# Attention scores: VectorE subtracts for all eight heads, ScalarE takes one exponential per graph

## The chip, the cores and the metric

One Trainium2 chip, one core. The metric is the device time of one launch in microseconds (us). The kernel before was timed three times; the profile is of a fourth execution.

## What is computed

There are 128 graphs of 128 nodes with 128 channels each. A graph layer with attention comes first, then a mixture of experts; the change lies in the attention alone.

```python
q, k, v = (split_heads(layernorm(x) @ W + b) for W, b in ((Wq, bq), (Wk, bk), (Wv, bv)))   # 8 heads of 16
scores = einsum('bhqd,bhkd->bhqk', q, k) / 4
scores = where(adj[:, None] > 0, scores, -9e15)
attn = softmax(scores, axis=-1)
x = x + (attn @ v, heads joined) @ Wo + bo
x = x + ffn(layernorm(x))        # a shared expert and the best two of eight others
```

## The kernel before

The program has five phases, one behind the other: attention, router, shared expert, routed experts, and a last one that adds the pairs up. The attention phase goes over 128 tiles, one graph each, in 32 rounds of four tiles (`GT = 4`; tile `t = 4g + j`). Every engine has its own list of work, written out by hand in a `step(g, q)` of its own, and the lists meet at semaphores only. Within an engine the order is fixed.

For one tile the work goes like this. TensorE writes the negated scores of eight heads into the four banks of S (L736) and adds the mask with four more matmuls (L739), which raises `s_ps`. VectorE takes the minimum per head (L474, `softmax_shift`, L470) and then subtracts the scores from it for the first `SHIFTED = 6` heads, from PSUM into `probs` in SBUF (L477), which raises `sub_done`. ScalarE computes the other two heads straight from S, one exponential each with the minimum as bias (L621, `direct_done`), and then exponentiates the six shifted heads in place (L626, `exp_done`). TensorE turns the eight blocks in two halves (L750, L766) into the one bank of PT, which ScalarE copies out after each half (L612, L616), and multiplies by V (L778); ScalarE copies the sums (L629), TensorE turns them (L759), and VectorE divides by the denominators (`normalise`, L457).

There is one S. TensorE's step for the next tile begins with the scores into S, and waits for `sub_done` and `direct_done` of the tile before (L732, L733).

Around this each round of four tiles carries other work, at a fixed place behind the subtraction of one of its tiles. On VectorE: at j = 0 `normalise` and the statistics of a later group (`stats1`, `gather1`); at j = 1 `residual` and `choose`; at j = 2 `normalise` and `mask` (L455, the mask of the next group); at j = 3 `place` (L504, whose first product L507 raises `slot_terms`), `stats2` and `gather2`. On TensorE: `aT` at j = 0, `out` at j = 1, Q and K at j = 2, V and the router's logits (`lg`, L705) at j = 3. At j = 3 the product with V waits for `slot_terms`, since the ranks share its bank. On ScalarE: copies of `aT`, Q, K, V and the logits. GpSimd (POOL) normalises rows (L297 and L301 among others) and sends rows to their slots.

Of the kernel before, what the change touches and what calls it, by code (L numbers as in the profile page):

```python
# [20 lines left out]
VW = 2 * HD  # L21
HH = H // 2
NEG = -9000000000000000.0
SHIFTED = 6
EPS = 1e-5
E = 8
EA = E + 1
# [24 lines left out]
def attention_phase(nc, ctx, d, x_res, x_rows, row_words, logits, rt, row_sent, xT_dram, slots_dram):  # L52
# [7 lines left out]
    def sem(name):  # L60
# [69 lines left out]
             "k_ps", "k_sb", "v_ps", "v_sb", "aT_ps", "aT_sb", "out_ps", "x2_done", "bn2_done", "aggr2", "rs1_done", "rs2_done", "ve1_done", "ve2_done", "xc1_done", "xc2_done",  # L130
             "xs2_done", "hi_done", "split_done", "x2T_in", "lg_ps", "lg_sb",
             "top_done", "eq_done", "keyed", "key_done", "pick_done", "rest_done", "rank_ps", "counted", "slot_terms", "slot_ready",
             "s_ps", "min_done", "sub_done", "direct_done", "exp_done", "pt_ps", "pt_sb", "pv_ps", "o_sb", "on_ps", "rec_done", "norm_done"]
    s = {n: sem(n) for n in names}

    def wait(eng, name, count):
# [228 lines left out]
    def _(dve):  # L365
# [104 lines left out]
        def softmax_shift(t, b):  # L470

            wait(dve, "s_ps", t + 1)
            wait(dve, "sub_done", t)
            dve.tensor_reduce(smin[:].rearrange("p (r e) -> p r e", e=2), S_heads, AX_X, ALU.min).then_inc(s["min_done"], 1)  # L474
            wait(dve, "min_done", t + 1)
            wait(dve, "pt_ps", 2 * (t - 1))
            dve.tensor_tensor(probs[:, b, 0:SHIFTED].rearrange("p (r e) k -> p r e k", e=2),  # L477
                              smin[:, 0:SHIFTED].rearrange("p (r e) -> p r e", e=2).unsqueeze(3).to_broadcast([P, SHIFTED // 2, 2, P]),
                              S_heads[:, 0:SHIFTED // 2], ALU.subtract).then_inc(s["sub_done"], 1)

        def choose(g, q):

# [80 lines left out]
    @nc_block.scalar  # L563
    def _(act):
        act.wait_ge(prep, 8)

        def high_half(g):
            wait(act, "xn_ready", g + 1)
            wait(act, "xnT_in", g * GT * 16)
            act.activation(xn16[:, :, 0], xn[:], ACT.Copy).then_inc(s["xhi_done"], 1)  # L570

        def evac(task, g, q):
            if task == "Q":
                wait(act, "q_ps", g + 1)
                act.activation(QT[:, q], M0[:, :], ACT.Identity, bias=qb[:], scale=-0.25 / (XS * WS)).then_inc(s["q_sb"], 1)
            elif task == "K":
                wait(act, "k_ps", g + 1)
                for e in range(2):
                    last = act.activation(KT[:, q, e], M0[:, :], ACT.Identity, bias=kb[:, e:e + 1], scale=parity_s[:, e:e + 1])
                last.then_inc(s["k_sb"], 1)  # L580
            elif task == "V":
                wait(act, "v_ps", g + 1)
                act.activation(V[:, q, :, :, 0:HD].rearrange("p j h c -> p (j h) c"),
                               M0[:, :].rearrange("p (j c) -> p j c", c=HD), ACT.Copy,
                               scale=1.0 / (XS * WS)).then_inc(s["v_sb"], 1)
            elif task == "aT":
                wait(act, "aT_ps", g + 1)
                act.activation(attnT[:], last_bank(g, task)[:, :], ACT.Copy).then_inc(s["aT_sb"], 1)
            elif task == "lg":
                set_up(act, g)  # L590
                wait(act, "lg_ps", g + 1)
                act.activation(logits[:, bass.ds(g * GT, GT), :], M0[:, 0:GT * E].rearrange("p (j e) -> p j e", e=E),
                               ACT.Copy, scale=1.0 / (XS * WS)).then_inc(s["lg_sb"], 1)

        def keep_transposed(t, half):
            wait(act, "pt_ps", 2 * t + half + 1)
            if half == 0:
                wait(act, "pv_ps", t - 1)
            return PT[:, :, :]

        def step(g, q):
            for j in range(GT):
                t = g * GT + j
                b = {0: ("lg", g - 4, q), 1: None, 2: ("Q", g + 1, 1 - q), 3: ("K", g + 1, 1 - q)}[j]
                a = {0: ("aT", g - 2, q), 1: None, 2: None, 3: ("V", g + 1, 1 - q)}[j]
                if isinstance(g, int) and g == -1 and j == 0:
                    high_half(0)
                    high_half(1)
                if b and has(b[1]):
                    evac(*b)  # L610
                if has(t, 1, NT):
                    act.activation(pT[:, (j - 1) % 2, 0:HH], keep_transposed(t - 1, 0), ACT.Copy).then_inc(s["pt_sb"], 1)  # L612
                if a and has(a[1]):
                    evac(*a)
                if has(t, 1, NT):
                    act.activation(pT[:, (j - 1) % 2, HH:H], keep_transposed(t - 1, 1), ACT.Copy).then_inc(s["pt_sb"], 1)  # L616
                if has(t, 0, NT):
                    wait(act, "min_done", t + 1)
                    wait(act, "pt_ps", 2 * (t - 1))
                    for h in range(SHIFTED, H):  # L620
                        last = act.activation(probs[:, j % 2, h], S_heads[:, h // 2, h % 2], ACT.Exp,  # L621
                                              bias=smin[:, h:h + 1], scale=-1.0)
                    last.then_inc(s["direct_done"], 1)
                    wait(act, "sub_done", t + 1)
                    pr = probs[:, j % 2, 0:SHIFTED]
                    act.activation(pr, pr, ACT.Exp).then_inc(s["exp_done"], 1)  # L626
                if has(t, 2, NT):
                    wait(act, "pv_ps", t - 1)
                    act.activation(oT[:], OD[:, 0:2 * P].rearrange("p (a t) -> p a t", a=2), ACT.Copy).then_inc(s["o_sb"], 1)  # L629
                if j == 3 and has(g, -2) and not (isinstance(g, int) and g < 0):  # L630
                    high_half(g + 2)

        def drain():
            evac("lg", NG - 4, 0)
            act.activation(pT[:, 1, 0:HH], keep_transposed(NT - 1, 0), ACT.Copy).then_inc(s["pt_sb"], 1)
            evac("aT", NG - 2, 0)
            act.activation(pT[:, 1, HH:H], keep_transposed(NT - 1, 1), ACT.Copy).then_inc(s["pt_sb"], 1)
            for t in (NT - 2, NT - 1):
                wait(act, "pv_ps", t + 1)
                act.activation(oT[:], OD[:, 0:2 * P].rearrange("p (a t) -> p a t", a=2), ACT.Copy).then_inc(s["o_sb"], 1)  # L640
            evac("aT", NG - 1, 1)
            for g in range(NG - 3, NG):
                evac("lg", g, g % 2)

        pair_blocks(act, step)
        drain()

    @nc_block.tensor
    def _(pe):
# [10 lines left out]
        def m0_task(task, g, q, step_g):  # L660
# [15 lines left out]
            elif task == "aT":  # L676
                wait(pe, "norm_done", (g + 1) * GT // 2)
                bank = last_bank(g, task)
                if bank is not M0:
                    wait(pe, "sub_done", NT)  # L680
                    wait(pe, "direct_done", NT)
                else:
                    m0_free(pe, task, step_g)
                for j in range(GT):
                    mm = pe.transpose(bank[:, j * P:(j + 1) * P], attn[:, q, j].rearrange("p h c -> p (h c)"), ident[:])
                mm.then_inc(s["aT_ps"], 1)
            elif task == "out":
                wait(pe, "aT_sb", g + 1)
                bank = last_bank(g, task)
                if bank is M0:  # L690
                    m0_free(pe, task, step_g)
                pe.matmul(bank[:, :].rearrange("p (j c) -> p j c", j=GT), sel[:],
                          bias3[:].unsqueeze(1).to_broadcast([P, GT, P]), start=True, stop=False)
                for j in range(GT):
                    mm = pe.matmul(bank[:, j * P:(j + 1) * P], attnT[:, j * P:(j + 1) * P], wo[:], start=False, stop=j == GT - 1)
                mm.then_inc(s["out_ps"], 1)
            elif task == "lg":
                rows_turned(pe, g)
                if isinstance(g, int) and g >= NG - 3:
                    wait(pe, "lg_sb", g)  # L700
                else:
                    m0_free(pe, task, step_g)
                for j in range(GT):
                    for n, (a, b) in enumerate(((0, 0), (0, 1), (1, 0))):
                        mm = pe.matmul(M0[:, j * E:(j + 1) * E], xT[:, q, a, j * P:(j + 1) * P],  # L705
                                       wr16[:, b], start=n == 0, stop=n == 2)
                mm.then_inc(s["lg_ps"], 1)
# [13 lines left out]
        def step(g, q):  # L721
            for j in range(GT):
# [4 lines left out]
                if has(t, 0, NT):  # L727
# [2 lines left out]
                        wait(pe, "k_sb", g + 1)  # L730
                        wait(pe, "mask_ready", g + 1)
                    wait(pe, "sub_done", t)  # L732
                    wait(pe, "direct_done", t)  # L733
                    for r in range(4):
                        rows = slice(32 * r, 32 * r + 32)
                        pe.matmul(S_heads[:, r], QT[rows, q, j * P:(j + 1) * P], KT[rows, q, :, j * P:(j + 1) * P],  # L736
# [835 lines left out]
```

## Time and profile before

| what | value |
|---|---|
| median of three runs | 1387.17 us (1382.49 to 1388.42) |
| the profiled execution | 1381.66 us, span 1379.8 us |
| PE, DVE, ACT, POOL busy over the whole span | 79%, 73%, 63%, 62% |
| first and last reduction of scores (L474) | 43.4 us and 657.9 us |

The attention phase is a little under half of the span. Shares over the whole span mix it with four phases that have other limits, so they tell little of it; the round of four tiles is the unit to look at, and the length of a step is the time from one reduction L474 to the next. In the rows, PE is TensorE, PEld its weight loads, DVE VectorE, ACT ScalarE. A bracket at the end of a row of the timeline gives how long the engine was idle before it, and what ended that.

### The profile page before, as it was taken

The page shows a single profiled execution, that of the slowest core. Times are in us where ns is not written, and L with a number is a line of the kernel's source. Part 1 is how long each engine was busy: PE and PEld are TensorE (multiplying, and loading weights), DVE is VectorE, ACT ScalarE, POOL GpSimd, SP SyncE. Part 2 cuts the span into 40 slices and gives each one's busy share as a digit, 9 for nine tenths or more (in the row PEclk, how much of TensorE's full clock was granted, in tenths as well). Part 3 has the DMA queues.
Part 4 walks back from the last instruction along what each step waited for, and adds up shares of the span by engine and source line. Part 5 has one row for each costly group of instructions (what it writes and reads, how often), then busy time and mean ns, then how long its engine had stood idle before and what let it go on. Part 6 is the DMA issues. An engine that isn't in the chain of part 4 may idle for free. (4 is left out here: it accounts for less than half of the span.)

```text
span 1379.8 us, 39795 instructions
## 1 busy us (share of the span) xinstructions
PE 1088.6 (79%) x12580; PEld 791.9 (57%) x12581; DVE 1010.7 (73%) x2407; ACT 866.9 (63%) x1705; POOL 856.1 (62%) x897
## 2 busy tenths in 40 slices
PE   0788888888888888888348999989999999989300
PEld 0456666666666666666226767757777777768200
DVE  3367777777877787777447798767777777757498
ACT  0577777777777777777236878766767676657200
POOL 3125676776667766675666777627777777766400
PEclk9999999999999999999769999999999999989755
DMA  2112333323333223322233545244444444423399
GB/s 74 25 45 65 84 82 84 92 67 82 84 87 81 76 79 86 82 67 49 70 98 102 164 147 156 77 80 103 97 101 97 90 101 96 88 63 77 113 337 307
DMA packets 276549, 136.54 MB, mean 99 GB/s; under 512 B 195142, under 2 KB 254700, under 8 KB 276474
## 3 DMA queue, kind: packets, MB, share of 16 engines
q1 hardware_dynamic: 242938, 93.39, 28.2%
q0 software_dynamic: 16896, 33.86, 7.7%
q10 hardware_dynamic: 16640, 8.39, 2.0%
q8 instruction: 34, 0.56, 0.2%
q14 instruction: 41, 0.34, 0.1%
HBM read 47.95 MB, written 54.04 MB: 74 GB/s over the span
## 5 line engine op out<-in xcount | busy, mean ns | idle before, releaser
L1376 POOL DMA_INDIRECT pairs_dram<-x_rows x272 | 278.9, 1025 | 124.5 <-issue 85.1
L1054 ACT ACTIVATE hid<-Z,biases 128x512 f32<-128x512 f32 (+1 forms) x336 | 208.1, 631 | 138.4 <-PE Z L1022 91.1
L474 DVE TENSOR_REDUCE smin<-S 128x8 f32<-128x1024 f32 x128 | 156.8, 1225 | 136.3 <-PE S L739 135.2
L1069 DVE SCALAR_TENSOR_TENSOR h<-hid,h 128x512 f16<-128x512 f32 (+1 forms) x288 | 183.7, 650 | 53.3 <-ACT h L1045 48.9
L1034 PEld LDWEIGHTS Y<-w,h 128*128 128x128 f16 x3168 | 186.0, 99 | 26.7 <-issue 10.6
L1034 PE MATMUL Y<-w,h 128*128 (+1 forms) x3168 | 193.0, 221 | 10.3 <-DVE h L1069 8.3
L1167 POOL DMA_INDIRECT slots_dram<-x_rows,pair_slot x128 | 132.7, 1036 | 46.0 <-issue 23.9
L1022 PE MATMUL Z<-x_rows,w 128*128 128x512 f16 (+1 forms) x720 | 150.2, 355 | 11.0 <-issue 8.8
L736 PE MATMUL S<-KT,QT 32*128 32x256 f32 x1024 | 93.0, 429 | 75.2 <-ACT probs L621 71.6
L335 POOL DMA_INDIRECT slots_dram<-x_rows,pair_slot x116 | 118.7, 1023 | 28.9 <-issue 23.4
L306 POOL TENSOR_TENSOR xn<-xn 128x512 f16<-128x512 f32 x32 | 37.0, 1156 | 159.9 <-ACT xn L570 159.9
L477 DVE TENSOR_TENSOR probs<-smin,S 128x768 f32<-128x768 f32 x128 | 122.1, 954 | 14.4
L616 ACT ACTIVATE pT<-PT 128x512 f32<-128x512 f32 x127 | 75.7, 596 | 71.1 <-PE PT L766 70.7
L1045 ACT ACTIVATE h<-hid 128x512 f16<-128x512 f32 (+1 forms) x176 | 105.8, 601 | 21.0 <-ACT hid L1054 5.4
L626 ACT ACTIVATE probs<-probs 128x768 f32<-128x768 f32 x128 | 109.3, 854 | 0.4 <-DVE probs L477 0.4
L1034 PE MATMUL Y<-w,x_rows 128*128 x1632 | 101.7, 220 | 6.7 <-DVE x_rows L1429 6.1
L1069 DVE SCALAR_TENSOR_TENSOR x_rows<-hid,x_rows 128x512 f16<-128x512 f32 (+1 forms) x160 | 97.1, 620 | 11.9 <-ACT x_rows L1045 8.9
L1034 PEld LDWEIGHTS Y<-w,x_rows 128*128 128x128 f16 x1632 | 96.6, 98 | 15.9 <-issue 8.6
L1022 PEld LDWEIGHTS Z<-x_rows,w 128*128 x720 | 66.7, 100 | 65.7 <-issue 16.9
L612 ACT ACTIVATE pT<-PT 128x512 f32<-128x512 f32 x127 | 76.5, 603 | 43.7 <-PE PT L750 43.7
L736 PEld LDWEIGHTS S<-KT,QT 32*128 32x128 f32 x1024 | 44.3, 185 | 101.1 <-issue 63.6
L1429 DVE SCALAR_TENSOR_TENSOR x_rows<-Y,logits 128x512 f32<-128x512 f32 (+1 forms) x80 | 48.9, 612 | 66.2 <-DMA pairs_dram<-x_rows 50.3
(212 smaller groups left out, 2244.7 us busy)
## 6 DMA issues: line engine op xcount, KB each, us to landing
y_pairs<-pairs_dram SPq DMA_DIRECT2D x32, 512.0 KB, 6.1
x_res<-in_x_dram SPq DMA_DIRECT2D x32, 256.0 KB, 3.3
adj<-in_adj_dram SPq DMA_DIRECT2D x32, 256.0 KB, 2.9
xT_dram<-xT SPq DMA_DIRECT2D x32, 256.0 KB, 3.3
xTu<-xT_dram SPq DMA_DIRECT2D x32, 256.0 KB
out_dram<-x_res ACTq DMA_DIRECT2D x16, 512.0 KB, 10.8
pairs_dram<-x_rows POOLq DMA_INDIRECT x272
slots_dram<-x_rows,pair_slot POOLq DMA_INDIRECT x256
```

The source lines that it names most:

```text
L335: pool.indirect_dma_start(slots_dram, bass.IndirectOffsetOnAxis(ap=rt.pair_slot[:, g * GT + j, 0:1], axis=0), row_words[:, g * GT + j, :], ...
L474: dve.tensor_reduce(smin[:].rearrange("p (r e) -> p r e", e=2), S_heads, AX_X, ALU.min).then_inc(s["min_done"], 1)
L477: dve.tensor_tensor(probs[:, b, 0:SHIFTED].rearrange("p (r e) k -> p r e k", e=2), smin[:, 0:SHIFTED].rearrange("p (r e) -> p r e", e=2).u ...
L626: act.activation(pr, pr, ACT.Exp).then_inc(s["exp_done"], 1)
L736: pe.matmul(S_heads[:, r], QT[rows, q, j * P:(j + 1) * P], KT[rows, q, :, j * P:(j + 1) * P], start=True, stop=False)
L1022: mm = pe.matmul(self.bank(b, c)[:, 0:w], self.w1[:, k, :, c * P:(c + 1) * P][:, e, :], self.xT[:, b, m, 0:w], start=n == 0, stop=n == 2)
L1034: mm = pe.matmul(self.Y[:, b % 2, j], self.piece(b)[:, k, c, j * P:(j + 1) * P], self.w2[:, m, :, c][:, e, :], start=c == 0 and n == 0, st ...
L1045: act.activation(self.piece(b)[:, 0, c, 0:w], self.hid[:, c, 0:w], ACT.Copy, scale=HS).then_inc(self.hi_done, 1)
L1054: act.activation(self.hid[:, c, 0:w], self.bank(b, c)[:, 0:w], ACT.Gelu, bias=bias[:, c:c + 1], scale=1.0 / (XS * WS)).then_inc(self.gelu_ ...
L1069: dve.scalar_tensor_tensor(out=self.piece(b)[:, 1, c, 0:w], in0=self.hid[:, c, 0:w], scalar=HS, in1=self.piece(b)[:, 0, c, 0:w], op0=ALU.m ...
L1167: pool.indirect_dma_start(slots_dram, bass.IndirectOffsetOnAxis(ap=rt.pair_slot[:, t, k:k + 1], axis=0), row_words[:, t, :], None).then_in ...
L1376: pool.indirect_dma_start(pairs_dram, bass.IndirectOffsetOnAxis(ap=pair_of[n][:, j:j + 1], axis=0), y_sb[n % NY][:, j], None, bounds_check ...
```

## The change

The two direct exponentials go. VectorE subtracts all eight heads in one instruction, ScalarE exponentiates all eight in place in one instruction, and TensorE's next scores wait for `sub_done` alone.

```diff
-SHIFTED = 6
...
-            dve.tensor_tensor(probs[:, b, 0:SHIFTED].rearrange("p (r e) k -> p r e k", e=2),
-                              smin[:, 0:SHIFTED].rearrange("p (r e) -> p r e", e=2).unsqueeze(3).to_broadcast([P, SHIFTED // 2, 2, P]),
-                              S_heads[:, 0:SHIFTED // 2], ALU.subtract).then_inc(s["sub_done"], 1)
+            dve.tensor_tensor(probs[:, b].rearrange("p (r e) k -> p r e k", e=2),
+                              smin[:].rearrange("p (r e) -> p r e", e=2).unsqueeze(3).to_broadcast([P, 4, 2, P]),
+                              S_heads, ALU.subtract).then_inc(s["sub_done"], 1)
...
-                    wait(act, "min_done", t + 1)
-                    wait(act, "pt_ps", 2 * (t - 1))
-                    for h in range(SHIFTED, H):
-                        last = act.activation(probs[:, j % 2, h], S_heads[:, h // 2, h % 2], ACT.Exp,
-                                              bias=smin[:, h:h + 1], scale=-1.0)
-                    last.then_inc(s["direct_done"], 1)
                     wait(act, "sub_done", t + 1)
-                    pr = probs[:, j % 2, 0:SHIFTED]
+                    pr = probs[:, j % 2]
                     act.activation(pr, pr, ACT.Exp).then_inc(s["exp_done"], 1)
...
                     wait(pe, "sub_done", t)
-                    wait(pe, "direct_done", t)
```

## Rows read from the trace of the kernel before

**Rows 1.** Page, part 1: busy us, share of the span, instructions of each engine.
```profile
PE 1088.6 (79%) x12580; PEld 791.9 (57%) x12581; DVE 1010.7 (73%) x2407; ACT 866.9 (63%) x1705; POOL 856.1 (62%) x897
```

**Rows 2.** Windows, 70 us of attention: busy us by engine, PEclk, DMA share.
```profile
280.00:350.00 70.00, 58.98 (x713) 42.47 (x710) 55.47 (x146) 51.09 (x112) 51.63 (x57) 1.00 0.30 78
```

**Rows 3.** Waits, 100 to 560 us: waiter, releaser, us in total, times, longest.
```profile
POOL xn L306 <- ACT xn L570: 112.4, 24, 11.8
DVE smin L474 <- PE S L739: 71.2, 82, 2.2
...
PE S L736 <- ACT probs L621: 52.2, 73, 0.8
```

**Rows 4.** Timeline, tile j = 1 of one round: start us, us, engine, line, operation.
```profile
301.38 1.23 DVE L474 TENSOR_REDUCE smin<-S 128x8 f32<-128x1024 f32 x1 [0.27 <-PE S L739]
...
302.74 0.96 DVE L477 TENSOR_TENSOR probs<-smin,S 128x768 f32<-128x768 f32 x1
...
303.58 0.60 ACT L616 ACTIVATE pT<-PT 128x512 f32<-128x512 f32 x1 [1.17 <-PE PT L766]
...
304.07 0.62 ACT L621 ACTIVATE probs<-S,smin 128x128 f32<-128x128 f32 x2
...
304.57 0.85 ACT L626 ACTIVATE probs<-probs 128x768 f32<-128x768 f32 x1
...
304.84 0.71 PE L736 MATMUL S<-KT,QT 32*128 32x256 f32 x8 [0.72 <-ACT probs L621]
...
306.13 1.23 DVE L474 TENSOR_REDUCE smin<-S 128x8 f32<-128x1024 f32 x1 [0.49 <-PE S L739]
```

**Rows 5.** Timeline, the next three reductions: tiles j = 3, 0 and 1.
```profile
311.37 1.23 DVE L474 TENSOR_REDUCE smin<-S 128x8 f32<-128x1024 f32 x1 [1.97 <-PE S L739]
...
316.33 1.23 DVE L474 TENSOR_REDUCE smin<-S 128x8 f32<-128x1024 f32 x1 [0.86 <-PE S L739]
...
320.74 1.22 DVE L474 TENSOR_REDUCE smin<-S 128x8 f32<-128x1024 f32 x1
```

**Rows 6.** Timeline, TensorE's way from tile j = 3 to the next round.
```profile
313.59 0.18 DVE L507 TENSOR_TENSOR eq<-OD,pick 128x32 f32<-128x32 f32 x1
...
313.92 0.64 PE L778 MATMUL OD<-pT,V 128*32 128x128 f32 x16 [0.31 <-DVE eq L507]
...
314.50 0.46 PE L705 MATMUL M<-wr,xT 128*128 128x8 f16 x12
...
315.04 0.71 PE L736 MATMUL S<-KT,QT 32*128 32x256 f32 x8
...
316.13 0.60 PE L750 MATMUL PT<-ident,probs 128*128 128x128 f32 x4
```

**Rows 7.** Timeline, the mask of two rounds beside GpSimd's subtraction.
```profile
308.98 0.42 DVE L455 TENSOR_SCALAR negmask<-adj 128x512 bf16<-128x512 f32 x1
309.01 1.29 POOL L297 TENSOR_TENSOR xn<-x_res,mv 128x512 f32<-128x512 f32 x1
...
328.29 1.03 POOL L297 TENSOR_TENSOR xn<-x_res,mv 128x512 f32<-128x512 f32 x1
328.34 1.27 DVE L455 TENSOR_SCALAR negmask<-adj 128x512 bf16<-128x512 f32 x1
```

**Rows 8.** Line L455: duration in ns, min/median/max, first and last start us.
```profile
L455 DVE TENSOR_SCALAR negmask<-adj x32: 396/420/1345, 22.5 to 637.2; 128x512 bf16<-128x512 f32 x32
```

**Rows 9.** Groups by form, VectorE, 100 to 560 us: busy us, mean ns | idle before.
```profile
L474 DVE TENSOR_REDUCE smin<-S 128x8 f32<-128x1024 f32 x95 | 116.3, 1225 | 72.2 <-PE S L739 71.2
L477 DVE TENSOR_TENSOR probs<-smin,S 128x768 f32<-128x768 f32 x96 | 91.6, 954 | 12.1
L465 DVE TENSOR_TENSOR attn<-ON,rden 128x256 f32<-128x256 f32 x48 | 20.4, 425 | 2.7
...
L434 DVE TENSOR_TENSOR x_res<-M,x_res 128x512 f32 x23 | 15.7, 684 | 0.0
```

**Rows 10.** Groups by form, ScalarE, the whole span.
```profile
L626 ACT ACTIVATE probs<-probs 128x768 f32<-128x768 f32 x128 | 109.3, 854 | 0.4 <-DVE probs L477 0.4
L1045 ACT ACTIVATE h<-hid 128x512 f16<-128x512 f32 x152 | 95.8, 630 | 17.8 <-ACT hid L1054 4.2 <-PE Z L1022 1.3 <-DVE x_rows L1069 0.3
...
L1045 ACT ACTIVATE h<-hid 128x256 f16<-128x256 f32 x24 | 10.0, 417 | 3.3 <-ACT hid L1054 1.2 <-DVE x_rows L1069 0.4 <-PE Z L1022 0.2
```

More of the change, by code:

```diff
@@ L132, in attention_phase @@
              "top_done", "eq_done", "keyed", "key_done", "pick_done", "rest_done", "rank_ps", "counted", "slot_terms", "slot_ready",
-             "s_ps", "min_done", "sub_done", "direct_done", "exp_done", "pt_ps", "pt_sb", "pv_ps", "o_sb", "on_ps", "rec_done", "norm_done"]
+             "s_ps", "min_done", "sub_done", "exp_done", "pt_ps", "pt_sb", "pv_ps", "o_sb", "on_ps", "rec_done", "norm_done"]
     s = {n: sem(n) for n in names}
@@ L680, in m0_task @@
                     wait(pe, "sub_done", NT)
-                    wait(pe, "direct_done", NT)
                 else:
```

## The prediction

> **What bounds the kernel now.** I read the shares first, only to set them aside: over the whole span TensorE is the busiest engine, with 79% [rows 1], but that is a mean over five phases. In a stretch of attention the engines stand closer: of 70 us TensorE is busy 58.98, VectorE 55.47, ScalarE 51.09, at a granted clock of 1.00, the higher of its two levels [rows 2]. No engine is full, so the order of the waits decides. The view of the waits names two: VectorE's reduction waits for scores (71.2 us in 460), and TensorE's scores wait for ScalarE's direct exponentials (52.2 us, 73 times of some 95) [rows 3].
>
> The timeline shows how these two hang together. In tile j = 1 the subtraction ends at 303.70 (302.74 + 0.96). ScalarE is then still in its second copy of PT, so the direct exponentials begin at 304.07 and end at 304.69, and the next scores begin at 304.84, after TensorE has stood still for 0.72 us [rows 4]. S is thus held for a whole microsecond after VectorE has finished with it, for two heads on an engine that was late. The scores and the mask need 1.29 us from start to reduction (304.84 to 306.13) [rows 4].
>
> One round from the reduction of j = 1 to the next one of j = 1 takes 19.36 us (301.38 to 320.74), in steps of 4.75, 5.24, 4.96 and 4.41 [rows 4, 5]; 95 reductions in 460 us give the same 4.84 a tile [rows 9]. Before them VectorE is idle 0.49, 1.97, 0.86 and not at all [rows 4, 5]: in the step from j = 0 to j = 1 VectorE is already full, in the other three the scores come late.
>
> **The cost of the parts.** VectorE's subtraction goes from 768 to 1024 columns. VectorE's two-tensor operations with one operand in PSUM take 0.425 us for 256 columns, 0.684 for 512 and 0.954 for 768 [rows 9], so another 256 cost 0.26 to 0.27: I take 0.27, a duration of 1.22. Removing the two direct exponentials takes 0.50 us of ScalarE's time per tile (304.07 to 304.57, when the next one starts) [rows 4]. The in-place exponential grows by 256 columns: 0.21 us by the step from 0.417 to 0.630 [rows 10], so 1.06 to 1.07 against 0.854. ScalarE gains 0.29 a tile; VectorE loses 0.27.
>
> By sums alone that would be a poor trade, since VectorE is the fuller of the two [rows 2]. The Trainium skill says as much (Perfetto Trace Analysis, Identifying the Most-Contended Engine): for VectorE, ScalarE and GpSimd the engine with the highest occupancy is the one to relieve first, and this change loads it instead. By that rule the sum is the loss alone; it returns below as a rival.
>
> What counts here is when S comes free. It is released at 302.74 + 1.22 = 303.96 where it was released at 304.69. From a finish on ScalarE to the scores it is 0.15 us (304.69 to 304.84) [rows 4], and from a finish on VectorE to a matmul also 0.15 (313.77 to 313.92) [rows 6]. So the scores could start at 304.11, and TensorE's own work was over at 304.12: the wait of 0.72 goes. I walk the four steps with that, each as the longest of its ways:
>
> - j = 0 to 1, now 4.41: VectorE had no idle time [rows 5], so it grows by the subtraction, to 4.68.
> - j = 1 to 2, now 4.75 with 0.49 idle [rows 4]: VectorE's own work is 4.26, then 4.53. The way over S is shorter: 1.36 (reduction to subtraction) + 1.22 + 0.15 + 1.29 = 4.02. So 4.53.
> - j = 2 to 3, now 5.24 with 1.97 idle [rows 5]: VectorE's own work 3.27, then 3.54; the way over S 4.02. So 4.02, the large gain.
> - j = 3 to 0, now 4.96 [rows 5]: here no direct exponential holds TensorE. It waits for the first product of `place`, which stands behind the subtraction: 2.22 from the reduction to L507, 0.18 for it, 0.15, 0.58 to the logits, 0.54 to the scores, 1.29 to the reduction, which is 4.96 [rows 5, 6]. The longer subtraction pushes all of it, to 5.23: a loss.
>
> Together 18.46 against 19.36, 0.90 less in a round. With 31 rounds (the first fills the pipeline) that is 28 us; I take off 2 for rounds at both ends, which lack some of this work: 26 us.
>
> What covers the rest: the single exponential can begin when ScalarE's copy lets it (304.07) and is done by 305.14; the first half of the turns follows the scores by 1.09 us (315.04 to 316.13) [rows 6], so it would begin at 304.12 + 1.09 = 305.21. The cover is thin, 0.07 us. Should it go, the turns are late by what is missing, but the reduction of the next tile has its scores by then and feels it only a tile later. Nothing of the change touches a DMA queue or GpSimd's list; the phases behind attention begin earlier and stay as they are.
>
> **The rivals.**
>
> *The mask hits GpSimd in every round.* VectorE's mask takes 0.42 us when it starts just ahead of GpSimd's L297 and 1.27 just behind it (308.98 against 309.01, 328.34 against 328.29) [rows 7]; over the phase 0.396 to 1.345 [rows 8]. Today that falls into the 1.97 us of idle time and costs nothing. With the change that step has only 4.02 - 3.54 = 0.48 to spare, so a mask of 1.27, 0.85 longer, costs 0.37 a round, or 11 us in all: 1372. For it: VectorE's longer steps put the mask later behind L297, which hangs on ScalarE. Against it: caught later, it waits only for the rest of L297, and up to 0.48 is free. The Trainium skill (GPSIMD Engine Reference, Specifications) says that GpSimd shares its SBUF interfaces with VectorE and that the two contend for some kinds of VectorE instruction; the trace agrees, with 0.42 against 1.27.
>
> *VectorE is the bound throughout.* If VectorE's work sets the pace in all four steps, as it does at j = 0, the change is a loss of 0.27 in each of 128: 34 us, 1421. This is where the skill's rule on occupancy leads. It decides as soon as an earlier release of S does not shorten a step, for instance where the subtraction of four full banks costs more than its columns: by the walk, where three of the four steps carry the subtraction with full weight and the fourth at least as much, the gain of 0.90 is used up when the subtraction grows by some 0.49 instead of 0.27. Against it: 71.2 us of VectorE's waiting for scores [rows 3], and the even spacing of 0.425, 0.684, 0.954 [rows 9].
>
> *Something else paces the round.* GpSimd's list or a DMA could hold the round at 19.36, and the time stays within 0.5% of 1387. Against it: GpSimd waits 112.4 us for ScalarE in 24 rounds, 4.7 each [rows 3], far more than the 0.90 to be saved.
>
> **How the numbers follow.** The profiled execution took 1381.66 us, 5.5 below the median of the three runs; minus 26 it would be 1356. Against the median the same gain gives 1361, which I predict. The forecast has a chance of 0.68, the mask 0.18, another pace 0.07, VectorE throughout 0.07. The range starts at 1349, where each step is 0.1 us shorter than walked (128 x 0.1 = 12 us), and reaches to 1379, past the mask's 1372 by about the scatter of the three runs (6 us), rounded up; outside it lie mainly the last two cases. A measurement of this kernel can tell 0.5%, 7 us, from no change. The forecast and the mask's case are both beyond that: faster 0.86, same 0.08, slower 0.06.
>
> **What would show it.** The waits after should have no row of scores behind ScalarE. The subtraction should read 1.22 us and the exponential 1.06. The steps should read about 4.68, 4.53, 4.02 and 5.23, and VectorE's idle time before L474 should remain at j = 2 and 3 alone. A step from j = 2 of 4.4 with masks over 1 us means the first rival; steps that are all longer by 0.27 mean the second; a round of 19.3 with new idle time everywhere the third. If TensorE's first turns wait for the exponential by more than a tenth, the thin cover was misjudged.

## The result, and the profile after

| | before | changed |
|---|---|---|
| median of the runs | 1385.81 us (4 runs, 1382.49 to 1388.42) | 1342.44 us (4 runs, 1339.24 to 1347.07) |
| ratio, 95% interval | | 0.9691 (0.9654 to 0.9727) |
| profiled execution, span | 1381.66 us, 1379.8 us | 1339.24 us, 1337.4 us |
| first to last reduction of scores | 43.4 to 657.9: 614.5 us | 43.7 to 621.1: 577.4 us |
| last reduction to the first add of the last phase | 649.0 us | 643.4 us |

The change makes the kernel faster, as forecast, but by 43 us where 26 were forecast; 1342 lies below the range. Of the 42 us between the two profiled executions 37 lie in the attention. The other 6 lie behind it, where nothing was changed; further profiles, below, show that they are the spread from one execution to the next.

First the shares: the page's part 1 of the changed kernel (to be held against [rows 1]), and a stretch of 70 us of attention in its windows (against [rows 2]; the columns are PE, PEld, DVE, ACT, POOL, each with its count, then PEclk, DMA share, GB/s).

```profile
PE 1092.7 (82%) x12580; PEld 782.3 (58%) x12581; DVE 1044.6 (78%) x2407; ACT 836.3 (63%) x1449; POOL 850.1 (64%) x897
```

```profile
280.00:350.00 70.00, 64.36 (x776) 44.69 (x773) 62.24 (x159) 51.36 (x89) 52.38 (x58) 1.00 0.32 86
```

VectorE went from 55.47 to 62.24 busy of 70 and TensorE from 58.98 to 64.36, at the same granted clock. ScalarE has lost a part of its work per tile and is as busy as before, since the tiles come faster.

The waits of the changed kernel, 100 to 540 us (waiter, releaser, us in total, times, longest), answer to [rows 3]:

```profile
POOL xn L305 <- ACT xn L569: 91.4, 25, 10.6
...
PEld S L727 <- DVE probs L476: 32.9, 70, 1.7
...
DVE smin L473 <- PE S L730: 22.8, 30, 1.8
...
PE S L727 <- DVE probs L476: 12.2, 44, 1.5
```

No row is left of scores that wait for ScalarE. VectorE's wait for scores fell from 71.2 us to 22.8. The groups by form of the same stretch give the two durations that the change grew (against [rows 9, 10]):

```profile
L476 DVE TENSOR_TENSOR probs<-smin,S 128x1024 f32<-128x1024 f32 x97 | 118.5, 1222 | 12.3
...
L619 ACT ACTIVATE probs<-probs 128x1024 f32<-128x1024 f32 x97 | 102.5, 1057 | 9.5 <-DVE probs L476 7.7 <-issue 0.2
```

1.222 and 1.057 us were forecast as 1.22 and 1.06. So the prices were right, and what was wrong lies in the walk through the steps. The timeline of one round, with the reductions of j = 0, 1, 2, 3 and the next j = 0, shows each of them (against [rows 4 to 6]):

```profile
410.12 1.22 DVE L473 TENSOR_REDUCE smin<-S 128x8 f32<-128x1024 f32 x1 [0.80 <-PE S L730]
...
411.48 1.22 DVE L476 TENSOR_TENSOR probs<-smin,S 128x1024 f32<-128x1024 f32 x1
...
412.73 1.06 ACT L619 ACTIVATE probs<-probs 128x1024 f32<-128x1024 f32 x1 [0.16 <-DVE probs L476]
...
412.75 0.71 PE L727 MATMUL S<-KT,QT 32*128 32x256 f32 x8 [0.24 <-DVE probs L476]
...
413.92 0.65 PE L741 MATMUL PT<-ident,probs 128*128 128x128 f32 x4
...
414.43 0.28 DVE L426 BATCH_NORM_AGGREGATE mv<-bn 128x2 f32<-128x6 f32 x3
...
414.63 1.19 DVE L473 TENSOR_REDUCE smin<-S 128x8 f32<-128x1024 f32 x1
...
419.11 1.22 DVE L473 TENSOR_REDUCE smin<-S 128x8 f32<-128x1024 f32 x1
...
420.46 1.22 DVE L476 TENSOR_TENSOR probs<-smin,S 128x1024 f32<-128x1024 f32 x1
...
421.74 0.71 PE L727 MATMUL S<-KT,QT 32*128 32x256 f32 x8
...
422.23 0.81 DVE L454 TENSOR_SCALAR negmask<-adj 128x512 bf16<-128x512 f32 x1
...
423.04 1.23 DVE L473 TENSOR_REDUCE smin<-S 128x8 f32<-128x1024 f32 x1
...
425.53 0.18 DVE L506 TENSOR_TENSOR eq<-OD,pick 128x32 f32<-128x32 f32 x1
...
425.86 0.64 PE L769 MATMUL OD<-pT,V 128*32 128x128 f32 x16
...
426.44 0.46 PE L697 MATMUL M<-wr,xT 128*128 128x8 f16 x12
...
426.82 0.71 PE L727 MATMUL S<-KT,QT 32*128 32x256 f32 x8
...
428.12 1.23 DVE L473 TENSOR_REDUCE smin<-S 128x8 f32<-128x1024 f32 x1 [0.70 <-PE S L730]
```

The steps of this round are 4.51, 4.48, 3.93 and 5.08. Rounds of two kinds alternate, and the program's loop holds two rounds. The table has means over 22 rounds in the middle of the phase (the 7th to the 28th), worked out from the starts of the reductions:

| step from | before | forecast | changed | changed, two kinds |
|---|---|---|---|---|
| j = 0 | 4.41 | 4.68 | 4.42 | 4.51 and 4.33 |
| j = 1 | 4.75 | 4.53 | 4.58 | 4.49 and 4.66 |
| j = 2 | 5.24 | 4.02 | 4.08 | 3.94 and 4.23 |
| j = 3 | 4.93 | 5.23 | 5.12 | 5.08 and 5.15 |
| round | 19.32 | 18.46 | 18.19 | 18.02 and 18.37 |

A round gains 1.13 us instead of 0.90, and j = 0 is the step that came out furthest below its forecast.

### The profile page after: what moved, and what is told of

Its sections match the earlier page's. It is cut to its first block and busy times, and to the rows that moved or that the text cites. A ratio compares the mean times of both kernels' runs of the same rounds, so it can differ in the third digit from the quotient of the medians.

```text
span 1337.4 us, 39286 instructions
## 1 busy us (share of the span) xinstructions
PE 1092.7 (82%) x12580; PEld 782.3 (58%) x12581; DVE 1044.6 (78%) x2407; ACT 836.3 (63%) x1449; POOL 850.1 (64%) x897
## 5 line engine op out<-in xcount | busy, mean ns | idle before, releaser
L1367 POOL DMA_INDIRECT pairs_dram<-x_rows x272 | 274.6, 1010 | 121.2 <-issue 87.4
L476 DVE TENSOR_TENSOR probs<-smin,S 128x1024 f32<-128x1024 f32 x128 | 156.3, 1221 | 14.4
L619 ACT ACTIVATE probs<-probs 128x1024 f32<-128x1024 f32 x128 | 135.2, 1057 | 15.4 <-DVE probs L476 13.0
L769 PE MATMUL OD<-pT,V 128*32 128x128 f32 x2016 | 81.2, 278 | 7.4 <-DVE eq L506 5.8
L757 PE MATMUL PT<-ident,probs 128*128 128x128 f32 x508 | 78.9, 278 | 5.6 <-ACT pT L611 2.6
```

Source lines behind the costliest of these rows:

```text
L476: dve.tensor_tensor(probs[:, b].rearrange("p (r e) k -> p r e k", e=2), smin[:].rearrange("p (r e) -> p r e", e=2).unsqueeze(3).to_broadca ...
L1367: pool.indirect_dma_start(pairs_dram, bass.IndirectOffsetOnAxis(ap=pair_of[n][:, j:j + 1], axis=0), y_sb[n % NY][:, j], None, bounds_check ...
```

## The experiments

**The kernel before and the changed kernel, once more.** No edit. These are for the 6 us behind the attention.

> The kernel before, once more, for a second profile. Attention (first to last reduction) took 614.5 us before and 577.4 after the change; the routed experts (first scores of that phase to the first add of the last phase) 404.6 and 398.0. Theory 1: the 6.6 us in the routed experts are the spread from execution to execution; then this execution's routed stretch lies anywhere from 397 to 406 and its attention again at 614 to 615. Theory 2: they belong to the program; then the routed stretch is 404 to 405 here, and about 398 in every kernel made from the changed one.

> The changed kernel once more, timed in five rounds beside the kernel before, with a second profile. Theory 1 (all that the change gains lies in the attention, 37 us; what the phases behind it showed on top is spread from execution to execution): the routed stretch lies anywhere from 397 to 408 us in this profile, and the ratio comes out at 0.970 to 0.975. Theory 2 (the routed stretch is shorter in the changed kernel): 398 again, and a ratio of 0.969 or less.

| profiled execution | first to last reduction | last reduction to the first add |
|---|---|---|
| before | 614.5 | 649.0 |
| before_again | 614.5 | 655.0 |
| changed | 577.4 | 643.4 |
| after_again | 577.4 | 652.1 |

The attention repeats to 0.1 us. The rest does not: 649 and 655 in one kernel, 643 and 652 in the other. Nearly all of that is the routed experts, 404.6 and 407.6 us before against 398.0 and 406.4. The 407.6 is 1.6 above what theory 1 allowed, and further from theory 2. In five rounds the changed kernel took 1348.02 us against 1383.13 (ratio 0.9735, 0.9712 to 0.9758): 35 us, inside theory 1's interval. The other profiles below settle it, since all their kernels are made from the changed one: the routed stretch took 404.3, 404.5, 405.1 and 400.2 us in four of them, and 398.6 and then 406.1 in two executions of one and the same (place_first and place_first_timed). Theory 2 wanted about 398 in all of them. So the gain is the attention's 37 us, and the first comparison showed some 6 more by chance.

The waits of the routed stretch say where the spread arises: VectorE waits until rows sent by GpSimd have left the buffer. First the execution with 398.0 us, then the one with 406.4, both from 866.5 to 1264.5 us (waiter, releaser, us in total, times, longest):

```profile
DVE x_rows L1420 <- DMA pairs_dram<-x_rows: 25.3, 29, 2.8
```

```profile
DVE x_rows L1420 <- DMA pairs_dram<-x_rows: 55.2, 44, 4.1
```

Why these transfers take longer in one execution than in another was not tried.

**Six heads only (six_only).** VectorE's and ScalarE's instructions are as wide as in the kernel before (768), and the direct exponentials are gone. The probabilities of the last two heads are a constant, written once.

```diff
+        dve.memset(probs[:, :, 6:H], 0.125)
...
-            dve.tensor_tensor(probs[:, b].rearrange(...), smin[:]..., S_heads, ALU.subtract)
+            dve.tensor_tensor(probs[:, b, 0:6].rearrange(...), smin[:, 0:6]..., S_heads[:, 0:3], ALU.subtract)
...
-                    pr = probs[:, j % 2]
+                    pr = probs[:, j % 2, 0:6]
```

> The changed kernel, but VectorE subtracts and ScalarE exponentiates six heads only; the probabilities of the other two are a constant, so a quarter of the softmax is left out. Theory 1 (the reduction of j = 1 was itself waiting for scores in the kernel before, though its row shows no idle time; VectorE's own work at j = 0 was 4.05 to 4.25): each step is 0.27 below the changed kernel's, 4.05 to 4.25 at j = 0, 4.2 to 4.4 at j = 1, 3.7 to 3.95 at j = 2, 4.8 to 4.9 at j = 3, a round of 16.8 to 17.4. Theory 2 (as predicted, VectorE's own work at j = 0 is 4.41): the step from j = 0 is 4.4.

Measured: 4.15, 4.27, 3.80, 4.85 (means over the same 22 rounds), a round of 17.07, 1313.36 us. At j = 0 the two kinds are 4.06 and 4.24. Its timeline, VectorE alone, the longer kind:

```profile
285.15 1.23 DVE L474 TENSOR_REDUCE smin<-S 128x8 f32<-128x1024 f32 x1 [0.78 <-PE S L731]
286.52 0.95 DVE L477 TENSOR_TENSOR probs<-smin,S 128x768 f32<-128x768 f32 x1
...
289.20 0.28 DVE L427 BATCH_NORM_AGGREGATE mv<-bn 128x2 f32<-128x6 f32 x3
289.39 1.19 DVE L474 TENSOR_REDUCE smin<-S 128x8 f32<-128x1024 f32 x1
```

The reduction follows 0.19 us after the start of the last aggregations; in the changed kernel it is 0.20 (414.43 to 414.63). In the kernel before it came 0.36 after, at 320.74 [rows 5], as two more rows of that timeline show:

```profile
319.45 0.71 PE L736 MATMUL S<-KT,QT 32*128 32x256 f32 x8 [0.72 <-ACT probs L621]
...
320.38 0.28 DVE L427 BATCH_NORM_AGGREGATE mv<-bn 128x2 f32<-128x6 f32 x3
```

The scores of that tile began at 319.45, and 319.45 + 1.29 is 320.74. So the reduction waited for the scores here too; the idle time, 0.08 us by these rows (320.38 + 0.28 to 320.74), was too small for the view to name it. Theory 1 holds, and the reading that VectorE was full at j = 0 falls.

This run also parts the change in two. Without the direct exponentials, and with the other instructions as wide as before, a round is 19.32 - 17.07 = 2.25 shorter; the eight-head instructions take back 18.19 - 17.07 = 1.12, four times 0.28. The 2.25 are not the price of the earlier release alone, since ScalarE also has 0.50 us less to do for each tile here. No run parts these two.

**The release held back (hold_exp).** The scores wait for the exponential in place of the subtraction. All engines do the work of the changed kernel.

```diff
-                    wait(pe, "sub_done", t)
+                    wait(pe, "exp_done", t)
```

> The changed kernel with one wait exchanged: the next scores wait for the exponential (exp_done) in place of the subtraction; no engine's work differs. Theory 1 (the gain is the earlier release of S): the way over S is 1.36 + 1.22 + about 0.1 + 1.06 + 0.15 + 1.29 = 5.2 in every step, a round of 20.5 to 21, 70 to 90 us more than the changed kernel's 1342 and more than the kernel before. Theory 2 (the gain is ScalarE's lighter work): within 10 us of the changed kernel.

Measured: 5.02, 5.09, 5.57, 5.13, a round of 20.81, attention 662.1 us, 1430.85 us (the kernel before on the same chip, one run: 1392.32). One step in its timeline:

```profile
316.42 1.23 DVE L473 TENSOR_REDUCE smin<-S 128x8 f32<-128x1024 f32 x1 [0.71 <-PE S L730]
...
317.79 1.22 DVE L476 TENSOR_TENSOR probs<-smin,S 128x1024 f32<-128x1024 f32 x1
...
319.04 1.06 ACT L619 ACTIVATE probs<-probs 128x1024 f32<-128x1024 f32 x1 [0.16 <-DVE probs L476]
...
320.15 0.71 PE L727 MATMUL S<-KT,QT 32*128 32x256 f32 x8 [1.33 <-ACT probs L619]
...
321.44 1.23 DVE L473 TENSOR_REDUCE smin<-S 128x8 f32<-128x1024 f32 x1 [0.61 <-PE S L730]
```

The round is as long as expected. The step from j = 2 is not: it took 5.57 where 5.2 was expected, because the exponential comes late there. It began 0.61 us after the subtraction had ended at 308.34, behind ScalarE's second copy of PT:

```profile
307.12 1.22 DVE L476 TENSOR_TENSOR probs<-smin,S 128x1024 f32<-128x1024 f32 x1
...
308.45 0.60 ACT L615 ACTIVATE pT<-PT 128x512 f32<-128x512 f32 x1 [0.86 <-PE PT L757]
...
308.95 1.05 ACT L619 ACTIVATE probs<-probs 128x1024 f32<-128x1024 f32 x1
```

One later release costs 85 us of attention against the changed kernel (662.1 against 577.4), with no engine's work changed. So ScalarE's lighter load by itself brings no gain: with it, and with a late release, the kernel is slower than the one before. The moment at which S comes free decides. It is released later here than in the kernel before, so the run does not show that ScalarE's lighter load is worth nothing once the release is early.

**The mask earlier (mask_first).** In VectorE's step of j = 2 the mask goes ahead of `normalise`.

```diff
+                if j == 2 and has(g, -1):
+                    mask(g + 1, 1 - q)
                 if j % 2 == 0 and has(g, 1):
                     normalise((g - 1) * 2 + j // 2, g - 1, 1 - q, j)
-                if j == 2 and has(g, -1):
-                    mask(g + 1, 1 - q)
```

> The changed kernel with the mask of the next group ahead of normalise in the step of j = 2, 0.6 us earlier. Theory 1 (the mask's collision with GpSimd's L297 costs up to 0.3 in every second round): the mask takes 0.42 again, the step from j = 2 is 3.93 in all rounds, and the mean round falls from 18.19 by 0.1 to 0.2, 3 to 6 us in all. Theory 2 (the way over the copies of K on ScalarE stands right behind it): the mask is short, but the step from j = 3 grows by as much, and the round stays within 0.1.

Measured: the step from j = 2 is 3.92 in both kinds of rounds, the round 18.02, attention 575.5 us, 1.9 less. The line's durations in ns (min/median/max), first in the profile of after_again, then here:

```profile
L454 DVE TENSOR_SCALAR negmask<-adj x32: 396/830/1291, 23.0 to 603.3; 128x512 bf16<-128x512 f32 x32
```

```profile
L454 DVE TENSOR_SCALAR negmask<-adj x32: 393/420/771, 22.5 to 598.8; 128x512 bf16<-128x512 f32 x32
```

So the collision of the mask with GpSimd, the first rival, does occur in most rounds of the changed kernel (its median is 0.83), but it costs only 0.29 in every second one. Theory 1 had the step and the round right; the whole phase gave 1.9 us where 3 to 6 were expected, since a few steps at the ends grew: in the second to last round the step from j = 2 took 5.68 against 4.24. Why was not followed up. The run was a single one, 1345.89 us, and its time cannot show that much.

**The first product of place ahead of the subtraction (place_first, place_first_timed).** At j = 3 VectorE multiplies ranks and picks between the reduction and the subtraction; `place_terms` is that first product, which raises `slot_terms`, and `place` is left with the rest.

```diff
         def softmax_shift(t, b, between=None):
...
             dve.tensor_reduce(smin[:]..., S_heads, AX_X, ALU.min).then_inc(s["min_done"], 1)
+            if between:
+                between()
             wait(dve, "min_done", t + 1)
...
-                    softmax_shift(t, j % 2)
+                    softmax_shift(t, j % 2, (lambda: place_terms(g - 4, q)) if j == 3 and has(g, 4) else None)
```

> The changed kernel with the first product of place moved from behind the subtraction of j = 3 to between its reduction and its subtraction. Theory 1 (the step from j = 3 is set by subtraction, place, the product with V, logits, scores): that product stops waiting for place, and the step from j = 3 falls from 5.08 to 5.16 by 0.15 to 0.25; 4 to 8 us off in all. Theory 2 (the copies of K on ScalarE set that step): TensorE's wait for K stays and the step stays within 0.1; no change in time.

> The changed kernel with the first product of place ahead of the subtraction, timed now. Its first profile gave a mean round of 17.87 against 18.19 and 570.5 us of attention against 577.4. Expected: the same stretch within 1 us, and 5 to 9 us less than the changed kernel, a ratio of 0.965 to 0.971 to the kernel before.

Measured: 1333.32 us in the single run. The step from j = 3 is 5.10 in the rounds where the step from j = 2 is 3.92, and 4.58 where that is 4.22: 4.84 in the mean, 0.27 less. The round is 17.87, the attention 570.5 and then 570.2 us, and timed the kernel takes 1342.97 us, a ratio of 0.970 (0.968 to 0.972), 5 us below the changed kernel on the same chip. The intervals of the two ratios overlap, so it is the attention stretch, 7 us shorter twice, that shows the gain. Theory 1 holds. The wait that theory 2 named comes next: V waits for the copies of K in both kinds of rounds, here in one with a step of 4.58 and then in one with 5.10, with the logits and the scores behind it:

```profile
347.38 0.84 PE L673 MATMUL M<-wv,xnT 128*128 128x128 f16 x12 [0.27 <-ACT KT L585]
...
349.17 0.46 PE L704 MATMUL M<-wr,xT 128*128 128x8 f16 x12
...
349.56 0.71 PE L734 MATMUL S<-KT,QT 32*128 32x256 f32 x8
```

```profile
365.11 0.84 PE L673 MATMUL M<-wv,xnT 128*128 128x128 f16 x12 [0.26 <-ACT KT L585]
...
366.90 0.46 PE L704 MATMUL M<-wr,xT 128*128 128x8 f16 x12
...
367.51 0.71 PE L734 MATMUL S<-KT,QT 32*128 32x256 f32 x8 [0.15 <-issue]
```

In the second kind V starts 1.41 us after the reduction instead of 1.11, since that reduction came 0.3 earlier. There the scores also follow the logits by 0.61 instead of 0.39, after idle time for which the profile names no other engine. This is where the program's loop of two rounds ends, and its last pass, which does not go back, takes 4.88 instead of 5.10. So the loop's end is the likely cause of some 0.2 us in every second round; no run tests it.

**The copies of K parted (place_first_k_split).** On top of the last edit, ScalarE's first copy of K goes between its two copies of PT at j = 2.

```diff
-  b = {..., 2: ("Q", g + 1, 1 - q), 3: ("K", g + 1, 1 - q)}[j]
-  a = {0: ("aT", g - 2, q), 1: None, 2: None, 3: ("V", g + 1, 1 - q)}[j]
+  b = {..., 2: ("Q", g + 1, 1 - q), 3: ("K1", g + 1, 1 - q)}[j]
+  a = {0: ("aT", g - 2, q), 1: None, 2: ("K0", g + 1, 1 - q), 3: ("V", g + 1, 1 - q)}[j]
```

> The kernel with place ahead of the subtraction, and ScalarE's two copies of K parted: the first between its two copies of PT at j = 2, the second at j = 3 where both were. Theory 1 (V waits for the second copy of K, 0.27 us a round, and through it the next scores): that wait goes, the step from j = 3 falls from 5.10 to 4.6 to 4.9 in the rounds where it was 5.10, the mean round from 17.87 to 17.6 to 17.8, 2 to 8 us off. Theory 2 (VectorE has nothing left to give): the wait goes and the round stays within 0.05.

Measured: the step from j = 3 is 4.74 and 4.35 (it was 5.10 and 4.58), the round 17.58, attention 559.9 us, and 1329.88 us timed, a ratio of 0.9618 (0.9602 to 0.9633). The wait for K, 6.8 us between 100 and 540 us in place_first, is gone from TensorE's waits. Theory 1, and more than it expected (attention 10 us shorter where 2 to 8 were expected), since both kinds of rounds gained. This version beats both kernels: 18 us below the changed one on the same chip.

## Why the prediction was wrong

- **S is the bound, and the direct exponentials hold it: right.** The wait of scores for ScalarE is gone, and hold_exp turns the gain into a loss by moving that one wait. Without the direct exponentials a round is 2.25 us shorter (six_only, which lightens ScalarE as well).
- **The prices: right.** 1.22 and 1.06 us, to the hundredth.
- **j = 0 "had no idle time, so it grows by the subtraction, to 4.68": this is the step that failed.** It is 4.42. In the kernel before, the reduction came when its scores did, 0.17 or 0.35 us later than VectorE's own work asked for: that needs 4.24 or 4.06 (six_only), and 4.51 or 4.33 with the longer subtraction. The missing bracket at 320.74 [rows 5] was read as proof that it was full. The same reduction one round earlier, the first of [rows 4], does name 0.27 us of idle time that scores ended: over the 22 rounds the idle time before it is 0.08 and 0.26 to 0.27 in turn, and the view names only the longer one. That is 0.26 a round, 8 us over 31 rounds.
- **j = 1, 4.53: right within 0.05** (4.58).
- **j = 2, 4.02: right in kind.** The way over S is 3.93, since the scores follow the subtraction by 0.06 us (421.68 to 421.74) and not by the 0.15 that was taken from the kernel before; in the other half of the rounds the mask makes it 4.23, as mask_first shows. The walk took VectorE's own work, 3.27, from a round with a mask of 0.42; already in the kernel before every second mask of these rounds took about 1.26 (one of them stands in [rows 7]), with idle time to take it in. The mean, 4.08, is 0.06 off.
- **j = 3, 5.23: the loss and its way were right, its size 0.11 too large** (5.12). Without the direct exponentials, and with the old widths, the step is 4.85 against 4.93, so some 0.08 of it hung on them. In every second round of the kernel before, the scores start 0.15 after the last direct exponential ends (295.53 to 295.68), as they do in the three other steps, so "no direct exponential holds TensorE" does not hold there. In the rounds between, as in [rows 4 to 6], the distance is 0.23 or more; the loop's end falls there, and what gave 0.08 in them too is open. The rest is that the walk started from a round of the longer kind, 4.96 against the mean of 4.93. A round of the shorter kind, from the kernel before:

```profile
294.90 0.63 ACT L621 ACTIVATE probs<-S,smin 128x128 f32<-128x128 f32 x2
...
295.23 0.46 PE L705 MATMUL M<-wr,xT 128*128 128x8 f16 x12
...
295.68 0.71 PE L736 MATMUL S<-KT,QT 32*128 32x256 f32 x8
```

- **The thin cover: right.** The exponential ends at 413.79 and the first turns start at 413.92, 1.17 us after the scores instead of 1.09. They are 0.08 late, less than the tenth that was named, and no step shows it.
- **Two us taken off for the rounds at both ends: wrong sign.** 31 rounds at 1.13 are 35 us, and the phase gained 37. The first round gained 2.7 us and the last two 1.9 and 1.5, not less than the others. Rounds that lack some of VectorE's work leave the release of S more to shorten; that is the likely reason, and no run tests it.
- **The total.** 0.23 more a round is 7 us, the ends are 4 more; that makes 37 of the 26. The measured 43 holds another 6 that belong to the spread of the routed experts, and the median of the kernel before was 1385.81 and no longer 1387.17. Walk and ends together, 11 us, used up nearly all of the 12 that the range left below 1361; the spread and the median carried the result past 1349. A gain of 37 from 1387.17 would have been 1350, at the very edge.
- **The rivals.** The mask does hit GpSimd, for 0.29 in every second round. The Trainium skill (GPSIMD Engine Reference, Specifications) names this contention, and the trace agrees, with 0.42 against 0.81 and 1.19. VectorE throughout did not come: it is by far the fuller of the two engines now, 62.24 of 70 against ScalarE's 51.36, and the kernel is faster. The rule of the Trainium skill (Perfetto Trace Analysis, Identifying the Most-Contended Engine), taken as this rival took it, led to the wrong sign here. Another pace did not hold the round, which fell from 19.32 to 18.19.

## What to carry to other kernels

When one buffer is handed round between engines, price a change by the moment at which the buffer is released, and only then by the sums of work: an engine with spare time can still be the one that releases late. A row without idle time does not prove that its engine is full: look at the same row in other rounds, and add up the other way into the same instruction (here 319.45 + 1.29 = 320.74); if both arrive together, the step can shrink. After the change walk the new longest way again, since two small reorderings on it gave half as much as the change itself.

## What the runs showed of the hardware

The scores followed the last exponential by 0.15 us when they waited for two semaphores (304.69 to 304.84), and the one event they wait for by 0.05 to 0.06 in the changed kernel and in hold_exp (421.68 to 421.74, 320.10 to 320.15). Whether the second wait costs the difference was not tried. The mask's 0.42 us became 0.81 or 1.19 beside GpSimd's subtraction of two SBUF tensors:

```profile
276.23 1.03 POOL L296 TENSOR_TENSOR xn<-x_res,mv 128x512 f32<-128x512 f32 x1
...
276.73 0.81 DVE L454 TENSOR_SCALAR negmask<-adj 128x512 bf16<-128x512 f32 x1
...
294.61 1.03 POOL L296 TENSOR_TENSOR xn<-x_res,mv 128x512 f32<-128x512 f32 x1
...
294.73 1.19 DVE L454 TENSOR_SCALAR negmask<-adj 128x512 bf16<-128x512 f32 x1
```

Both masks end 0.28 us after the subtraction does (277.54 against 277.26, 295.92 against 295.64), so the later a mask begins inside the subtraction, the less it loses. In the changed kernel 24 of the 32 masks began inside it, 0.03 to 0.69 us after its start, and all of them ended 0.28 to 0.29 after its end. In [rows 7] the mask that began first kept its 0.42, and the subtraction took 1.29 instead of 1.03.

Apart from the mask, `normalise` and the statistics at j = 0 differed by 0.19 between the two kinds of rounds, though the same instructions ran.
